# A two-layer Macaron block (MoE, recurrence, MoE): first FFN in two groups, its tiles fetched from x through an index table

## The reference

```python
def ffn(x):                                      # E = 8 experts, HD = 512
    probs = softmax(x @ router_w.T)
    mask = one_hot(argmax(probs), E)
    h = square(relu(einsum('btd,edh->ebth', x, expert_fc)))
    return einsum('ebtd,bte->btd', einsum('ebth,edh->ebtd', h, expert_proj), mask)

def rnn(x):
    step: h = tanh(x_t @ Wi.T + bi + h @ Wh.T + bh)
...
x = x + 0.5 * ffn(layernorm(x))
x = x + rnn(layernorm(x))
x = x + 0.5 * ffn(layernorm(x))
```

## Time and profile before

| | us |
|---|---|
| three runs | 616.0, 620.69, 633.88 |
| median | 620.69 |
| span of the profiled execution | 631.5 |
| first step, last step | 119.4, 549.7 |

### The profile page before, as it was taken

How to read it: one execution, slowest core, us unless ns; L and a number is a source line. 1 busy time by engine, 2 the same in 40 slices (tenths; PEclk the granted TensorE clock), 3 DMA queues, 4 the chain that set the end, 5 groups by cost and what they waited for, 6 DMA issues and landing times.

```text
span 631.5 us, 16046 instructions
## 1 busy us (share of the span) xinstructions
PE 584.7 (93%) x4831; PEld 566.4 (90%) x4831; DVE 392.7 (62%) x1418; ACT 347.2 (55%) x1189; POOL 309.9 (49%) x336
## 2 busy tenths in 40 slices
PE   1779999999999999999999999989999999997992
PEld 1659999999999999999999999979999998997992
DVE  3566678778557768778757756573334465684551
ACT  1245666676666666666566676621235653665671
POOL 1544478647718214387101677784322346365542
PEclk9999999999999999999999999985558999999997
DMA  6956663322313113233112533211211201326310
GB/s 204 255 184 203 228 205 94 92 78 68 100 49 81 48 56 97 82 99 117 40 40 59 161 98 106 70 43 50 82 37 43 77 27 68 111 77 180 105 45 6
DMA packets 57954, 60.99 MB, mean 97 GB/s; under 512 B 9463, under 2 KB 45314, under 8 KB 57872
## 3 DMA queue, kind: packets, MB, share of 16 engines
q1 hardware_dynamic: 47840, 38.77, 21.5%
q0 software_dynamic: 9440, 21.06, 10.3%
q10 hardware_dynamic: 592, 0.14, 0.1%
HBM read 28.59 MB, written 31.79 MB: 96 GB/s over the span
## 4 chain that ended last, share of the span: by engine, by line
PE 68%; POOL 11%; issue 8%; DVE 6%; DMA 3%; SPq 1%; ACT 1%; POOLq 0%; ACTq 0%; DVEq 0%
PE yp L1393 21%; PE hp L1380 19%; PE z L1403 9%; PE hp L1408 5%; PE mT L1298 5%; POOL back L954 5%; PE lg L1332 3%; PE xTp L1371 3%; POOL xs_dram L941 2%; PE z L1352 2%; DVE pay L1008 2%; POOL out_dram L960 1%; DMA bias<-in_L_attn_bh_dram 1%; DMA back<-ys_dram,pos 1%; POOL xs_dram L936 1%
## 5 line engine op out<-in xcount | busy, mean ns | idle before, releaser
L1393 PE MATMUL yp<-projT,s_sb 128*128 x1360 | 217.2, 291 | 2.7 <-ACT s_sb L1232 2.7
L1380 PE MATMUL hp<-xT_sb,w_sb 128*128 128x128 f32 x1360 | 213.2, 287 | 0.5 <-ACT w_sb L1223 0.5
L1203 ACT ACTIVATE hsT<-z 128x16 f32<-128x16 f32 x512 | 94.3, 184 | 176.3 <-PE z L1403 165.9
L1380 PEld LDWEIGHTS hp<-xT_sb,w_sb 128*128 128x128 f32 x1360 | 183.2, 199 | 1.0 <-issue 0.7
L1393 PEld LDWEIGHTS yp<-projT,s_sb 128*128 128x128 f32 x1360 | 176.3, 194 | 3.3 <-issue 3.1
L1403 PEld LDWEIGHTS z<-hsT,wT 128*128 128x128 f32 x1024 | 167.2, 202 | 11.8 <-ACT hsT L1203 3.0
L1403 PE MATMUL z<-hsT,wT 128*128 128x16 f32 x1024 | 163.7, 236 | 2.2 <-ACT hsT L1203 2.2
L1100 DVE TENSOR_SCALAR r_sb<-hp 128x512 f32<-128x512 f32 x170 | 116.8, 687 | 77.9 <-PE hp L1380 76.0
L1232 ACT ACTIVATE s_sb<-r_sb 128x256 f32<-128x256 f32 (+1 forms) x279 | 127.4, 457 | 44.6 <-DVE r_sb L1100 23.5
L1223 ACT ACTIVATE w_sb<-fc_sb 128x256 f32 (+1 forms) x279 | 129.0, 462 | 4.7 <-issue 2.3
L960 POOL DMA_INDIRECT out_dram<-y_sb,xs_sb x71 | 70.6, 994 | 85.1 <-DVE y_sb L1107 68.0
(11 more groups left out here) (106 smaller groups left out, 520.2 us busy)
## 6 DMA issues: line engine op xcount, KB each, us to landing
xs_sb<-xs_dram SPq DMA_DIRECT2D x71, 129.0 KB, 2.3
xs_sb<-xs_dram SPq DMA_DIRECT2D x99, 64.0 KB, 2.1
ys_dram<-y_sb SPq DMA_DIRECT2D x99, 64.0 KB
xs_dram<-zeros SPq DMA_DIRECT2D x12, 512.0 KB, 5.0
hsT<-in_L_attn_x_dram SPq DMA_DIRECT2D x16, 256.0 KB
hsT<-n_L_ffn_expert_proj_dram SPq DMA_DIRECT2D x1, 2048.0 KB, 9.1
fc_sb<-in_L_ffn_expert_fc_dram SPq DMA_DIRECT2D x1, 2048.0 KB, 20.3
xs_dram<-pay,pos POOLq DMA_INDIRECT x128, 2.6
```

The source lines that it names most:

```text
L1203: act.activation(state(t), z_step(t), ACT.Tanh).then_inc(s_h, 1)
L1380: mm = pe.matmul(hp[:, g % 2, h * P:(h + 1) * P], w_sb[:, g % 2, h * P:(h + 1) * P], xT_sb[:, g % 2, :], start=True, stop=True)
L1393: mm = pe.matmul(yp[:, 0:D], s_sb[:, g % 2, h, :], projT[:, bass.ds(offsets[g] + h * D, D)], start=(h == 0), stop=(h == HC - 1))
```

## The change

- FIRST is two groups, 4 and 12 units. Within a group tiles are listed by unit (by two units in the second, GRAIN): the tiles that a unit's tokens fill or begin come first. `tiles_before(u)` tells how many must be done before unit u can be gathered.
- No scatter in the first FFN. From the slots (`slots`, now eleven parts on DVE) one-hot matrices are built (`make_hot` on POOL, for every second unit of the first group on DVE; `make_eq` on DVE), and PE multiplies them (`make_index`) into a table of row numbers for every tile. Tiles are fetched from x in DRAM by indirect DMAs on POOL (`fetch`).
- The first FFN runs on raw x. Its mean is taken out of the weights: the router's and fc's rows are centred by a matmul with `level` = identity - 1/128 (`centre`), and the variance is applied after the product, since square(relu(a x)) = a^2 square(relu(x)): `scale` gives 0.5 / (var + eps), used in `add_back` and, for the second FFN, in `finish`. So norms and roots stay only in the middle.
- The host lays out x by rows and by columns, the weights transposed, and proj; no transposes of x, weights or proj on PE at the start. 16 `keep_warm` matmuls run first.
- MIDDLE has single units only; SECOND is [8, 1, 1, 3, 2, 1]; RING is 16; the planner's constants (PR) are others, hold among them (6.94 before, -180.4 after), and up to DEPTH = 4 tiles are ordered ahead. In beats with steps `finish` stands behind the side pieces on DVE.
- In `inputs` two matmuls of 256 columns replace four of 128.

```diff
-FIRST = [2, 2, 3, 4, 5]
-MIDDLE = [1, 1, 1, 1, 1, 1, 1, 1, 2, 1, 1, 3, 1]
-SECOND = [2, 2, 1, 3, 3, 1, 2, 1, 1]
-W = 2 * D + 2
-XN, XR, IDX, EXP = 0, D, 2 * D, 2 * D + 1
+FIRST = [4, 12]
+GRAIN = [1, 2]
...
-RING = 12
...
+RING = 16
...
+    def tiles_before(self, u):
+        v = (u - self.u0) // self.grain + 1
+        return min(UR * self.grain * v + E - 1, self.S)
...
+            def cols_in(i):
+                n0, n1 = i * COLS * UR, (i + 1) * COLS * UR
+                sp.dma_start(pay[:, n0:n1, 0:D], x_cols[:, n0 * P:n1 * P].rearrange("d (n p) -> d n p", p=P)).then_inc(s_cols[i], 16)
+            def fc_part(i):
+                w = E * HD // FCS
+                sp.dma_start(fc_sb[:, i * w:(i + 1) * w], fc_in[:, i * w:(i + 1) * w]).then_inc(s_fc[i], 16)
...
-                    sp.dma_start(xs_sb[:, g % RING, 0:D], xs1_dram[r.index][k * P:(k + 1) * P, :]).then_inc(s_load[g % RING], 16)
...
+            def make_hot(r, i):
+                u = hot_no(r, i)
+                pool.wait_ge(s_slots, slots_no[r.index])
+                if u >= HOTS:
+                    q, k = hot_before(r, i)
+                    pool.wait_ge(s_index, index_no[q.index, k])
+                if u == 0 or r.index and i == 0:
+                    pool.wait_ge(s_kc, 9)
+                for q in range(UR):
+                    n = u * UR + q
+                    pool.tensor_scalar(hot[:, u % HOTS, q, :], kio[:, :], slot_f[:, n:n + 1], ids[:, n:n + 1],
+                                       ALU.is_equal, ALU.mult).then_inc(s_hot, 1)
+            def fetch(g):
+                r, k = tiles[g]
+                if k == 0:
+                    pool.wait_ge(s_table, table_no[r.index])
+                if g >= RING:
+                    if is_second[g - RING]:
+                        put_landed(pool, g - RING)
+                    else:
+                        pool.wait_ge(s_tx, g - RING + 1)
+                pool.indirect_dma_start(
+                    out=xs_sb[:, g % RING, 0:D], out_offset=None, in_=x_rows.rearrange("p (n d) -> (p n) d", d=D),
+                    in_offset=bass.IndirectOffsetOnAxis(ap=index[:, r.index, k:k + 1].bitcast(U32), axis=0)).then_inc(s_fetch[g % RING], 16)
...
+            def scale(r):
+                J, n0 = r.J, r.n0
+                dve.wait_ge(s_stats, 4 * stats_no["stats", r.index, J // 4 - 1])
+                link(dve.tensor_scalar(double[:, 0:J], mv[:, int(r.second), n0:n0 + J, 1], 2.0, 2.0 * EPS, ALU.mult, ALU.add))
+                if r.second:
+                    dve.reciprocal(pay[:, n0:n0 + J, SCL:SCL + 1], double[:, 0:J].unsqueeze(2)).then_inc(s_scale, 1)
+                else:
+                    dve.reciprocal(scales[:, n0:n0 + J], double[:, 0:J]).then_inc(s_scale, 1)
...
+                rk4 = rk[:, 0:J, :].rearrange("p (v i) e -> p v i e", v=V)
+                pw4 = posw[:, 0:J, :].rearrange("p (v i) e -> p v i e", v=V)
+                own4 = own[:, 0:J, :].rearrange("p (v i) e -> p v i e", v=V)
+                rows = lambda a: a[:, 0:V, :].unsqueeze(2).to_broadcast([P, V, n, E])
+                sums = count[:, (nu - 1).bit_length() % 2, :, :]
                 if part == 0:
                     dve.wait_ge(s_rank, rank_no[r.index])
-                    link(dve.tensor_tensor(cmp[:, :, 0:J], rk3[:, J, :].unsqueeze(2).to_broadcast([P, E, J]),
-                                           thr[:, 0:J].unsqueeze(1).to_broadcast([P, E, J]), ALU.is_gt))
-                    link(dve.tensor_reduce(ntile[:, :], cmp[:, :, 0:J], AX_X, ALU.add))
-                    link(dve.tensor_tensor(tmp8[:, :, :], lower[:, :, :], ntile[:, :].unsqueeze(1).to_broadcast([P, E, E]), ALU.mult))
-                    link(dve.tensor_reduce(first_tile[:, :], tmp8[:, :, :], AX_X, ALU.add))
-                    link(dve.tensor_tensor(end_tile[:, r.index, :], first_tile[:, :], ntile[:, :], ALU.add))
+                    link(dve.tensor_copy(count[:, 0, PAD:PAD + nu, :], bank(r)[:, J * E:(J + nu) * E].rearrange("p (u e) -> p u e", e=E)))
+                    for i in range((nu - 1).bit_length()):
+                        a, d = count[:, i % 2, :, :], 1 << i
+                        link(dve.tensor_tensor(count[:, 1 - i % 2, PAD:PAD + nu, :], a[:, PAD:PAD + nu, :], a[:, PAD - d:PAD + nu - d, :], ALU.add))
+                elif part == 1:
+                    ends = sums[:, PAD:PAD + nu, :].rearrange("p (v g) e -> p v g e", g=r.grain)[:, :, r.grain - 1, :]
+                    link(dve.tensor_scalar(cum_i[:, 0:V, :], ends, float(P - 1), None, ALU.add))
+                    link(dve.tensor_scalar(begun[:, 1:V + 1, :], cum_i[:, 0:V, :], 7, None, ALU.arith_shift_right))
+                    link(dve.tensor_tensor(fresh1[:, 0:V, :], begun[:, 1:V + 1, :], begun[:, 0:V, :], ALU.subtract))
+                    link(dve.tensor_reduce(listed1[:, 0:V], begun[:, 0:V, :], AX_X, ALU.add))
+                elif part == 2:
+                    link(dve.tensor_tensor(tmp1[:, 0:V, :, :], lower[:, :, :].unsqueeze(1).to_broadcast([P, V, E, E]),
+                                           fresh1[:, 0:V, :].unsqueeze(2).to_broadcast([P, V, E, E]), ALU.mult))
+                elif part == 3:
+                    link(dve.tensor_reduce(begin1[:, 0:V, :], tmp1[:, 0:V, :, :], AX_X, ALU.add))
+                    link(dve.tensor_tensor(begin1[:, 0:V, :], begin1[:, 0:V, :], listed1[:, 0:V].unsqueeze(2).to_broadcast([P, V, E]), ALU.add))
+                    link(dve.tensor_tensor(end1[:, 0:V, :], begin1[:, 0:V, :], fresh1[:, 0:V, :], ALU.add))
+                elif part == 4:
+                    link(dve.scalar_tensor_tensor(out=open1[:, 1:V + 1, :], in0=fresh1[:, 0:V, :], scalar=0.0, in1=end1[:, 0:V, :],
+                                                  op0=ALU.is_gt, op1=ALU.mult))
+                    for v in range(2, V):
+                        link(dve.tensor_tensor(open1[:, v, :], open1[:, v, :], open1[:, v - 1, :], ALU.max))
...
+                elif part == 9:
+                    n1 = n0 + J
+                    link(dve.tensor_reduce(posf[:, 0:J], posw[:, 0:J, :], AX_X, ALU.add))
+                    dve.tensor_scalar(pos[:, 0, n0:n1], posf[:, 0:J], float(S * P - 1), None, ALU.min).then_inc(s_pos, 1)
+                    dve.wait_ge(s_pos, pos_no[r.index])
+                    link(dve.tensor_scalar(tile_i[:, 0:J], pos[:, 0, n0:n1], 7, None, ALU.arith_shift_right))
+                    link(dve.tensor_scalar(tile_f[:, n0:n1], tile_i[:, 0:J], 0.0, None, ALU.add))
+                    dve.scalar_tensor_tensor(out=slot_f[:, n0:n1], in0=tile_f[:, n0:n1], scalar=float(-P), in1=posf[:, 0:J],
+                                             op0=ALU.mult, op1=ALU.add).then_inc(s_slots, 1)
...
+                    link(dve.tensor_scalar(past[:, 0:V, :], end1[:, 0:V, :], lane[:, 0:1], None, ALU.is_le))
+                    link(dve.tensor_reduce(past_f[:, :], past[:, 0:V, :].rearrange("p v e -> p (v e)"), AX_X, ALU.add))
+                    link(dve.tensor_scalar(past_i[:, :], past_f[:, :], 0.0, None, ALU.add))
+                    dve.tensor_scalar(eoff[:, r.index:r.index + 1], past_i[:, :], E - 1, 9, ALU.bitwise_and,
+                                      ALU.logical_shift_left).then_inc(s_eoff, 1)
...
+            def make_eq(r, i):
+                u, S = hot_no(r, i), r.S
+                if u >= HOTS:
+                    q, k = hot_before(r, i)
+                    dve.wait_ge(s_index, index_no[q.index, k])
+                dve.tensor_tensor(eqt[:, u % HOTS, :, 0:S], kio[:, 0:S].unsqueeze(1).to_broadcast([P, UR, S]),
+                                  tile_f[:, u * UR:(u + 1) * UR].unsqueeze(2).to_broadcast([P, UR, S]), ALU.is_equal).then_inc(s_eq, 1)
+            def make_table(r):
+                dve.wait_ge(s_index, index_no[r.index, r.J // UR - 1])
+                dve.tensor_scalar(index[:, r.index, 0:r.S], bank(r)[:, 0:r.S], 0.0, None, ALU.add).then_inc(s_table, 1)
...
-                    dve.scalar_tensor_tensor(out=y_sb[:, g % RING, :], in0=yp[:, 0:D], scalar=0.5, in1=xs_sb[:, g % RING, XR:XR + D],
-                                             op0=ALU.mult, op1=ALU.add).then_inc(s_y, 1)
+                    dve.scalar_tensor_tensor(out=y_sb[:, g % RING, :], in0=yp[:, 0:D], scalar=xs_sb[:, g % RING, SCL:SCL + 1],
+                                             in1=xs_sb[:, g % RING, XR:XR + D], op0=ALU.mult, op1=ALU.add).then_inc(s_y, 1)
                 else:
-                    dve.tensor_scalar(y_sb[:, g % RING, :], yp[:, 0:D], 0.5, None, ALU.mult).then_inc(s_y, 1)
+                    dve.tensor_copy(y_sb[:, g % RING, :], yp[:, 0:D]).then_inc(s_y, 1)
             def add_back(u):
+                r = route_of[u]
                 dve.wait_ge(s_gath[u], 16 * UR)
-                v = pay[:, u * UR:(u + 1) * UR, XR:XR + D]
-                dve.tensor_tensor(v, raw(u).rearrange("p (j d) -> p j d", d=D), back[:, u % BACK, :, :], ALU.add).then_inc(s_add, 1)
-                dve.wait_ge(s_add, add_no[u])
```

(32 more changed lines are left out.)

881 lines of the change are left out of this document (498 added, 383 removed).

## The result

The changed kernel takes 634.9 us (median of four runs, 633.5 to 637.0), against 618.4 us for the kernel before (four runs, 608.1 to 633.9). The ratio is 1.036, with a 95% interval of 1.028 to 1.044: slower by 2.8 to 4.4%. It compares the fast runs of the two kernels alone, which is why it is not the quotient of the medians. The forecast was 573 us, in a range of 552 to 612, and faster. The profiled execution of after has a span of 631.8 us.

A forecast was written before the change was run, and what follows sets the result against it. The prediction took PE, busy for 93% of the span, as the bound. First step at 100 us, plus 512 x 0.67 and 98 x 0.56 gives 498; a tail of 73 makes 571, forecast as 573 us, range 552 to 612.

The forecast's parts named there:

- POOL: POOL's load: fits beside steps, hardly ahead of the first step; a one-hot's price, the unknown, taken as 0.4 us.
- the prediction's own formula: Group 1's index table: comes 48 x (t - 0.4) later if a one-hot on POOL costs t us.
- the 25 us of slack: Group 1's index table: may come until about 125 us; lateness beyond 25 us of slack delays all that follows.
- the rival "slower": POOL is the bound: with one-hots from 2.2 us on, the kernel is slower than 633 us; chance 0.05.
- the sum of 64 us in 62: POOL ahead of the first step: fetches, gathers, roots and one-hots need 64 us in the 62 there are.
- Start of the steps: Opening up to the first recurrence step: first y at 44 us, first step at 100, ends 88 and 112.
- the lone stretch: Steps without tiles while the second FFN's eight-unit group is prepared: 80 us, 278 to 358 us, at 0.67 a step.
- During the steps: The 512 recurrence steps with 98 tiles beside them: from 100 to 498 us.
- the model of 0.67 a step and 0.56 a tile: Recurrence: a lone step takes 0.67 us at full clock, and a tile beside steps adds 0.56 us.
- "the clock falls in the lone stretch": Rival: lone steps at 1.28 us for all 80 us, giving 619 us, or 596 for half; chance 0.25.
- Tail: After the last step: 28 tiles left, three fewer in the last stretch, last root and norm gone; 73 us.
- before's 29 us at half clock: Kernel before, 405 to 481 us: lone steps at 1.28 us cost 29 us, laid to the clock.

The follow-up runs named there:

- e10: The changed kernel in its own order, with each of group 1's 48 GpSimd one-hots made twice, one after the other: 676.1 us.
- e12: The kernel with one-hots on VectorE and group 1's scale placed earlier (618.4 us), its second FFN's first group of eight units split into two of four: 619.6 us.
- e22: The changed kernel with all one-hots on VectorE, new planner orders and the second FFN's eight-unit group split into two of four: 603.9 us, ratio 0.989 to the kernel before.

## Why the prediction was wrong

**The step that failed** is the one under *POOL*: "I take 0.4, by the row of equal shape". The affine select of 128x128 has one input and no per-partition scalar; the one-hot compares with one such scalar and multiplies by another, and takes 0.83 us. The other estimate, drawn out from L913, was 1.1, so the measured price lay inside the bounds. By the prediction's own formula (48 x 0.43) it makes the table 21 us later, which the 25 us of slack would have covered at no cost: the rival "slower" was set to begin at 2.2 us. That formula was wrong as well. It took the slack from a table that would otherwise be ready near 100 us. But the slots of group 1, which are 11 pieces on DVE in competition with everything else there, were ready only at 85.4 us; 48 one-hots of 0.83, four gathers and a root later it is 131. The doubled one-hots (+41 us) show that there was no slack left at all. Nor was POOL short of time as the sum of 64 us in 62 had it: it stood idle for 24 of them behind the slots, and then everything came at once. The 23 tiles that the prediction had done by the first step were 18, since the fetches of the last five stood behind the one-hots.

**Start of the steps, 123.7 instead of 100.** First transpose 45.4 (38, ends 33 to 46: inside), first y 59.6 (44), and from there to the first step 64 us (56). The 15.6 us at the first y are the clock's for the most part by an estimate: PE is busy for 28.7 of the 29.5 us from 29 to 58.5 us, at a granted clock of 0.50, and at the full clock this would be some 14 us less. No run measured it. I had counted what lies there at the full clock's price ("twice that if PE starts slowly" was for group 0's logits alone) and named the clock as a rival only in the lone stretch. The last 8 us are the one-hots', in two ways that no run parts. The root of unit 0 stood behind 16 of them: its statistics were done at 99.1, and it began at 107.4. And index units stand on PE ahead of the first step: the bias was added by 119.9, but PE then waited for one-hots and ran the unit of 121.93. With doubled one-hots (e10) the root moved by 22 us and the first step by 37; the index units are the rest.

**During the steps, 430 us instead of 398.** By the model of 0.67 a step and 0.56 a tile, 39 steps and 8 tiles from 123.6 to 175 us should take 31 us and took 51 (+20); 206 steps and 51 tiles to 345, 167 and took 170 (+3); 111 steps and 3 tiles to 430, 76 and took 85 (+9); 156 and 39 to the end, 126 and took 124 (-2). Three tiles more than forecast are the rest. So the price of steps and tiles held, and the first 51 us, starved of tiles and at half clock, are most of the miss. The 9 us in the lone stretch are explained below.

**The clock.** The rival "the clock falls in the lone stretch" had the mechanism, but the wrong place. In the lone stretch forecast for 278 to 358 us (it was 345 to 430) the full clock was held nearly throughout, and by the filling, as the run without it shows. It fell where PE waited for POOL between index units. From 103 to 153 us it stood at 0.51 with PE busy for 44.6 of 50 us:

```profile
29.00:58.50 29.50, 28.66 (x123) 0.50 0.17 53
...
103.00:153.00 50.00, 44.62 (x165) 0.51 0.10 16
```

The Trainium skill ("TensorE: Matmul & The Clock Gate", What's actually happening) says that activity releases the throttle. The lone stretch with and without filling (0.96 and 0.61) agrees with it. These 50 us, and those of before, don't: activity as the record counts it was there, without a break from 121.9 us on, and the full clock came only at about 154.5. The return of tiles does not explain it. With doubled one-hots the clock rose at 165.8 us, 7 us after PE's last wait, with only index units, steps and filling since, and the first tile's transpose there came at 190.5; and in before it stayed at 0.50 from 462 to 478 us with tiles running beside the steps. What releases the clock stays open.

**The lone stretch** itself did nearly as forecast: no tile from 350 to 400 us, 0.67 us a step at the full clock, and tiles back right after the 32nd scatter (417.7 us). But 65 steps in these 50 us make 0.77 each. From 350 to 355 us the clock stood at 0.50, after PE had waited 1.55 us for a y of DVE, and near 373 us the rank matmuls of the eight-unit group (L1541, 32 in 2.05 us) stood between two steps. So the rival did come true there too, for some 6 us. That the stretch costs nothing as such was implied by the sum, and e12 bears it out.

**Tail, 78.3 instead of 73,** with 30 tiles, not 28. Not looked into further.

**The base.** I laid before's 29 us at half clock to "the clock" and measured the forecast against 631.5. The change was then compared with runs near 615, so a part of the gain that I forecast had never been there to take. The kernel of e22, with its orders mended, its one-hots on VectorE and two groups of four, shows how much was right in the sum: 110.9 + 411 + 79 = 601 us against 100 + 398 + 73. The three terms are 11, 13 and 6 us off, the change is worth about 1%, and the sign of the forecast depended on where the one-hots are made and when one scale is ready.

Still open: what the opening's half clock costs (it is there in the best version too), and what an earlier table of group 1 would give: there the slots are ready at 85.7 us, and DVE makes the one-hots in fours between its other pieces until 123 us (64 of them, 18.0 us in all), so that the table comes at 127.2.

## What to carry to other kernels

Larger groups save padding tiles, but every list computed once for a group (here an index table and a scale) becomes a wait of the group's first member for the work of its last. Look for each of them in the code, and give each a due time of its own. An operation whose price has bounds of 0.3 to 1.1 us and which occurs 48 times in one queue ahead of the start is worth more thought than the other terms together: ask what else stands in that queue (here the root that releases the first step, and the fetches of the last five tiles of group 0), and what the starved engine's clock will do. Changing only one engine's share of a planned order can make things worse; move the work, then make the order anew, and only then judge.
